# At most two indirect DMAs in flight: the edge sort's scatters and the edge sums' gathers

## What is computed

```python
pre = jnp.power(jnp.clip(out_deg, 1.0), -0.5)[:, None]
h = feat * pre
agg = jax.ops.segment_sum(h[src], dst, num_segments=N_NODES)
rst = agg @ weight
```

```python
h = (x @ W.T).reshape(n, heads, out_ch)
e = jnp.exp(e - m[dst])
s = jax.ops.segment_sum(e, dst, num_segments=n)
alpha = e / (s[dst] + 1e-16)
out = jax.ops.segment_sum(alpha[:, :, None] * h[src], dst, num_segments=n)
```

## Time and profile before

| | us |
|---|---|
| median of 3 runs | 10622.69 |
| lowest and highest | 10619.56, 10624.97 |
| span of the profiled execution | 10685.8 |
| PE busy in it | 6666.1 (62%) |
| DVE busy | 5067.1 (47%) |
| POOL busy | 3649.9 (34%) |
| ACT busy | 2678.2 (25%) |

### The profile page before, as it was taken

One profiled execution on the slowest core, in us unless ns is written; L12 is line 12 of the kernel. 1 busy time (PEld: TensorE's weight loads), 2 busy tenths in 40 slices (PEclk: granted clock), 3 DMA queues, 4 the chain that ended last, 5 costly groups with the idle time before them and its releaser, 6 DMA issues. The chain is left out here.

```text
span 10685.8 us, 95917 instructions
## 1 busy us (share of the span) xinstructions
PE 6666.1 (62%) x27702; PEld 4202.5 (39%) x27702; DVE 5067.1 (47%) x10547; ACT 2678.2 (25%) x6047; POOL 3649.9 (34%) x3597
## 2 busy tenths in 40 slices
PE   5456656689657536649984663665664577626856
PEld 4452333334444433336753332333443233313434
DVE  6453046522477733461126544436545788733231
ACT  0012100022244404302223430331222455312211
POOL 2522346400246436602032763462111355120021
PEclk5558877799779857769996776677787799868968
DMA  3110033210246433304423333331022122210012
GB/s 94 38 34 13 4 89 91 56 46 27 69 136 179 120 98 88 91 6 131 168 83 96 95 90 78 101 91 32 15 67 61 44 68 69 68 58 7 7 60 76
DMA packets 440710, 758.91 MB, mean 71 GB/s; under 512 B 172573, under 2 KB 268795, under 8 KB 437521
## 3 DMA queue, kind: packets, MB, share of 16 engines
q0 software_dynamic: 182080, 437.26, 15.1%
q1 hardware_dynamic: 239987, 295.32, 8.8%
q10 hardware_dynamic: 18136, 20.19, 0.6%
HBM read 669.59 MB, written 82.56 MB: 70 GB/s over the span
## 5 line engine op out<-in xcount | busy, mean ns | idle before, releaser
L2448 POOL DMA_INDIRECT R<-table,edges x1248 | 1243.2, 996 | 861.0 <-issue 306.3
L2500 DVE TENSOR_TENSOR acc<-acc,PS 125x256 f32 (+3 forms) x1664 | 704.9, 424 | 1242.4 <-PE PS L2519 376.5
L2519 PE MATMUL PS<-R,hot 128*125 128x256 f32 (+1 forms) x1664 | 644.8, 476 | 418.0 <-issue 203.4
L2527 PE MATMUL PS<-iota_b,ident_b 128*128 128x500 bf16 x1728 | 764.7, 449 | 5.7 <-PEq L71 5.7
L2268 PE MATMUL PS<-S,hotT 125*128 125x100 bf16 (+1 forms) x6240 | 362.9, 218 | 575.1 <-DVE hotT L2375 460.4
L2460 ACT ACTIVATE R<-R,TW 128x128 f32<-128x128 f32 (+1 forms) x1248 | 493.4, 431 | 685.0 <-DMA R<-table,edges 644.7
L2519 PEld LDWEIGHTS PS<-R,hot 128*125 128x125 f32 x1664 | 361.6, 234 | 683.1 <-issue 520.3
L2517 PE MATMUL PS<-R,hot 128*125 128x258 f32 x1664 | 438.0, 416 | 203.6 <-DVE acc L2498 117.5
L2268 PEld LDWEIGHTS PS<-S,hotT 125*128 125x128 bf16 x6240 | 315.3, 112 | 623.8 <-DVE hotT L2375 429.7
L2448 POOL DMA_INDIRECT xx<-table,edges x416 | 412.8, 992 | 384.4 <-PE PS L2519 312.5
L2448 POOL DMA_INDIRECT room<-table,edges x416 | 425.6, 1023 | 330.2 <-PE PS L2519 191.7
(11 more groups left out here) (719 smaller groups left out, 13558.8 us busy)
## 6 DMA issues: line engine op xcount, KB each, us to landing
rowb<-slo_row SPq DMA_DIRECT2D x260, 250.0 KB
W<-in_L_ffn_W1p SPq DMA_DIRECT2D x32, 1024.0 KB
W<-in_L_ffn_W2p SPq DMA_DIRECT2D x32, 1024.0 KB
near<-dst_row SPq DMA_DIRECT2D x98, 256.0 KB
R<-table,edges POOLq DMA_INDIRECT x1248
W<-in_L_ffn_w SPq DMA_DIRECT2D x16, 1024.0 KB
hib<-hi_mask SPq DMA_DIRECT2D x260, 50.0 KB
g<-gate_rows POOLq DMA_DIRECT2D x8, 1568.0 KB
```

The costliest lines, as they stand in the source:

```text
L2448: pool.indirect_dma_start(self.R[:, u, 0:self.W], None, self.table[:, :], bass.IndirectOffsetOnAxis(ap=self.G.edges[:, g, 0:1], axis=0)).t ...
L2500: v.tensor_tensor(to, to, self.G.PS[0:P, self.bank + k, 0:self.WH], ALU.add).then_inc(self.put, 1)
L2519: mm = pe.matmul(self.G.PS[0:P, self.bank + k, 0:self.WH], hot, self.R[:, u, :], start=True, stop=True)
L2527: pe.matmul(G.PS[:, 6, 0:4 * P], G.ident_b[:, :], G.iota_b[:, :].unsqueeze(1).to_broadcast([128, 4, P]), start=True, stop=True)
```

## The change

Before scatter f (from the third on) POOL waits until scatter f - 2 has landed; for that the one semaphore becomes two that alternate. Before gather g (from the third of a sum on) POOL waits until gather g - 2 has landed, on the semaphore of that gather's slot. The wait for a free slot stays. SP waits for both scatter semaphores. The same instructions move the same data in the same order.

```diff
@@ class Scatter
-        self.scattered, self.fetched = s.sem("scattered"), s.sem("fetched")
+        self.scattered, self.fetched = [s.sem(f"scattered{j}") for j in range(2)], s.sem("fetched")
 
     def send(self, pool, f):
+        if f >= 2:
+            pool.wait_ge(self.scattered[f % 2], 16 * (f // 2))
         pool.indirect_dma_start(self.G.sorted[:, :], bass.IndirectOffsetOnAxis(ap=self.place[:, f:f + 1], axis=0),
-                                self.rows[:, f, :], None).then_inc(self.scattered, 16)
+                                self.rows[:, f, :], None).then_inc(self.scattered[f % 2], 16)
...
     def sync(self, sp):
-        sp.wait_ge(self.scattered, 16 * FE)
+        for j in range(2):
+            sp.wait_ge(self.scattered[j], 16 * len(range(j, FE, 2)))
@@ class EdgeSums, gather
         u = g % self.slots
         if g >= self.slots:
             pool.wait_ge(self.summed, g - self.slots + 1)
+        if g >= 2:
+            self.landed(pool, g - 2)
         pool.indirect_dma_start(self.R[:, u, 0:self.W], None, self.table[:, :],
                                 bass.IndirectOffsetOnAxis(ap=self.G.edges[:, g, 0:1], axis=0)).then_inc(self.got[u], 16)
```

## The result

The changed kernel takes 11229.35 us (median of 3 runs, 11214.6 to 11247.65) against 10622.69: a ratio of 1.057, 95% interval 1.055 to 1.059. It is 607 us slower; the forecast was +188, and the range ended at 11020. The profiled execution has a span of 11227.6 us, 542 us more than that of before.

What follows compares the result with a forecast made beforehand. The prediction took signals between engines, late while POOL issues without pause, as the bound. Terms +77 (narrow sums), +137 (sum 1), -26 (early gathers), 0 (scatters) gave +188 us on 10622.7: 10811 us, range 10440 to 11020.

Steps and rivals of the forecast that it cites:

- What bounds the kernel now: Sums and stages beside indirect DMAs: while POOL issues without pause, other engines' signals come late; 17.4 us per 12 gathers.
- Gathers with 1 KB rows: Sums 0, 2, 3, 4: two in flight give 1.50 us a gather, +77 us; ends -78 (1.40) and +232 (1.60).
- Sum 1: Gathers with rows twice as wide: 1.80 us each against 1.47, +137 us, between +87 and +170.
- Early gathers: 112 gathers issued ahead: a pace of 1.40 slows DVE less and POOL has slack; gain 26 us, ends 0 and 120.
- Scatters: Sort and late scatters: landing after 2.11 us meets the wait asked after 2.52 us, so pace and slowing stay; 0.
- Rival 4: Signals stay late with the wait on top of each pause; 1.60 a gather, 1.88 in sum 1; +402, 11025 us; chance 0.18.
- Rival 1: Signals come in time in the gathers, not in the scatters; -61 us, 10562 us; chance 0.18.
- Rival 2: Signals in time in the gathers, and scatters freed too, late ones and sort; about -207, 10416 us; chance 0.14.
- The estimate from the Trainium skill: Gather landings of 2.0 us plus bytes / 436e3: waits met almost before POOL comes, sum 1 would lose nothing.
- The prediction's sign of being wrong in its sign: Wrong in sign if PE beside the scatters or DVE beside the early gathers runs as fast as after them.

Runs made afterwards that it cites:

- late_scatters_paced: Kernel before plus a small POOL fill (256 columns) behind each late scatter, no landing wait; 10509.49 us, ratio 0.9895, where signals are late.
- the series above: POOL fills behind scatters against the kernel before, where signals are late: PE beside the late scatters 0.56, 1.28, 2.30 matmuls per us at 1.26, 1.35, 1.46 us.
- landing_first: Changed kernel with the two gather waits swapped, landing wait before slot wait; 10697.7 us, ratio 1.091 to the kernel before.
- whole_change: The changed kernel, unedited, on a chip where the kernel before has no late signals; 11054.11 us, ratio 1.128 to the kernel before.
- same_as_before: The kernel before, unedited, profiled on a chip without late signals; 9799.32 us, ratio 1.000.
- landing_first_no_spare: Changed kernel with landing wait before slot wait and no spare matmul behind each narrow sum; 10868.96 us, ratio 1.023 to the kernel before, where signals are late.

## Why the prediction was wrong, step by step

**"What bounds the kernel now"** held for the profiled execution, and its causal claim (signals come late by POOL's pace) was confirmed for the late scatters by late_scatters_paced and the series above. What it couldn't see is that this is not the kernel's nature: on four other chips the same program issues at the same pace with every signal in time.

**"Gathers with 1 KB rows"**: this is the step that failed most, +602 for +77. "With a little for POOL's restart I take 1.40" put 0.02 us where 0.72 was due. The prediction names no row for the restart, and none of before could show it, since every gather there has one wait at most and carries it itself. The change adds a second wait to each gather, the landing wait became an instruction of its own, and landing_first shows what that alone costs. With 2.76 + 0.72 a pair takes 3.48 us, and with the longer landings 1.82 to 1.86 a gather, above even the upper end of 1.60. The question on which the step spent its care, whether the signals would be late at 1.40, didn't arise: these sums take 2847 us here and 2843 on a chip without late signals, so at 1.8 they aren't.

**"Sum 1"**: the same term. Landing was right, 3.5 us (the median; the mean is 3.59); with the restart (3.59 + 0.72) / 2 is 2.16, measured 2.20, +302 for +137.

**"Early gathers"**: the mechanism was right, the size was not, -103 for -26, since their pace became 2.5 to 2.9 us and not 1.40 (116 us for 48 in sum 2): a pair takes 4.9 us there although these gathers carry their only wait themselves, and the landings recorded in that window have a mean of 4.6 us, beside the other DMAs of that stage, and the rows from inside sum 2 hadn't shown that. They do have the slack that was claimed.

**"Scatters"**: right for the 126 late ones (pace 1.26, PE still slow, +3 us), wrong for the sort, -159 for 0. The 2.11 us of the late scatters was taken as "the same instruction", but in the sort other DMAs run beside it, and there the landing is often longer: in whole_change, which is the changed kernel on another chip, the median is 2.5 us and one in ten takes 3.7 or more, against 2.1 for the late ones. From its trace:

```profile
163.55 0.96 POOL L1760 DMA_INDIRECT sorted_edges<-edge_rows,edge_place  x1 [0.92 <-DMA sorted_edges<-edge_rows,edge_place]
...
177.91 1.05 POOL L1760 DMA_INDIRECT sorted_edges<-edge_rows,edge_place  x1 [2.08 <-DMA sorted_edges<-edge_rows,edge_place]
```

These waits do bind. They free PE and DVE in the sort on a late chip (1844 matmuls for 1053 in the first 371 us, the same 1844 as in same_as_before) and cost 65 us on one without late signals.

**Not in the sum**: 94 us behind the last gathers. With late signals DVE had a backlog when the last gather of a sum was out; the earlier trace rows shows it being worked off. In sums 0 to 4 the last add ended 18, 30, 35, 22 and 29 us behind the last gather, after the change 6, 14, 6, 10 and 6: 91 of the 94 us.

**Rivals.** Rival 4, slower by more, had the sign, and its total of +402 was nearest; its mechanism (late signals plus a longer cycle) was not what happened, so that nearness is luck. Rival 1 had the signals right, in time in the sums and late beside the late scatters, and its price wrong by the same restart. Rival 2 was half there: freed in the sort and in the early windows, not beside the late scatters. The estimate from the Trainium skill ("DMA: Bandwidth & Descriptors", "Anatomy of one DMA — SWDGE (gpsimd) path"), landings of 2.3 and 2.6 us, was rightly not followed: 2.76 and 3.5 were measured.

The prediction's sign of being wrong in its sign (DVE beside the early gathers as fast as after them) nearly came, 2.3 against 2.5 per us, and yet the sign was right: it watched the gain, and the error was in the cost.

**Open.** What makes a chip one of the late kind, and what in it the issues and the signals share, no run shows. One suspect stands in the traces themselves, the recording of the profile. On the late chips most records of semaphore updates by DMAs are missing: the trace of the kernel before holds 28,517, that of same_as_before, the same program, 65,832. They are missing where the others are slow: between the first and the last late scatter 368 are there, 2032 in same_as_before, and 2001 in late_scatters_paced, where the same scatters 1.46 us apart disturbed nobody. Each execution on record has a granted clock, so each was recorded. Whether the recording holds the signals up, or both suffer from one cause, no run shows, and the times of a late chip without recording are not known. Releasers in the late chips' traces ("remote", "issue") are named from these incomplete records too; beside the late scatters most of PE's idle time is "issue" (78 of 103 us). That it is signals that come late is read from the earlier trace rows and inferred elsewhere.

Nor was it tried on a late chip whether the sort and the early gathers limited to two, with the late scatters paced, add up; on such a chip late_scatters_paced alone is the fastest kernel measured, on the others the kernel before is.

## What to carry to other kernels

When a change adds a second wait to an instruction, cost the restart behind a wait that stands alone, and put the wait that is met last where the instruction carries it itself; here the order of two lines was worth 356 us. A limit of n in flight sets a pace of (landing + restart) / n by the mean landing at that place, so take it from the same stage with the same traffic, and limit only where the stage has slack. Before believing the releasers of a trace, see whether its records are complete. Where a program's time differs by 8% between chips, a forecast from one profile holds for the kind of chip it was taken on.

## What the runs showed of the hardware

On two of the chips used for the experiments, and in the first profile, the other engines stand while POOL issues indirect DMAs back to back at 1.25 us: in sum 2 DVE stood 5.60 us for sums that PE had done, and beside the late scatters PE did 0.56 matmuls per us in place of 2.51. At 1.35 it did 1.28, at 1.46 2.30. On four other chips nothing of this shows at 1.25. A gather restarted 0.72 us behind a landing when the wait stood ahead as an instruction of its own, 0.23 us when it carried the wait. Three in flight with the landing wait last gave 1.36 to 1.41 us a gather, where the median landing and restart allow 1.16 and the kernel before takes 1.29 to 1.32; the median gap in these narrow sums stayed 1.25 to 1.27, so the second wait costs something at some gathers and not at each. The landing of a gather of 128 rows of 1 KB took 2.76 us (median) in the sums and some 4.6 to 5.5 (mean) in the early windows. PE's granted clock fell from 0.94 to 0.53 in the limited sum 0 (same_as_before and whole_change), near the 1.2 GHz level, and at 0.77 (landing_first) and 0.50 (landing_first_no_spare) that sum kept one pace, 1.60 and 1.61 us a gather.
